# Mixture of experts in a Perceiver kernel: routing of the first layer alone ahead of the tiles, the rest among them

## The reference, cut to what matters

```python
def _route_combine_weights(x_addr, U, k, tau):
    z = x_addr @ U.T
    topv, topi = jax.lax.top_k(z, k)
    w = jax.nn.softmax(topv / (tau + EPS), axis=1)
    ...
    return jnp.zeros((N, L), z.dtype).at[rows, topi].add(w)

def _mixture(inp, C, W):
    for e in range(L):
        y = y + C[:, e:e + 1] * (inp @ W[e].T)
    return y
...
xa = xf @ P_w.T
C1 = _route_combine_weights(xa, U1, K_ROUTE, TAU)
C2 = _route_combine_weights(xa, U2, K_ROUTE, TAU)
C3 = _route_combine_weights(xa, U3, K_ROUTE, TAU)
h = jax.nn.gelu(_mixture(xf, C1, W1), approximate=False)
y = _mixture(h, C2, W2) + C3 @ b2
```

## Time and profile before

| | us |
|---|---|
| three runs, median (lowest to highest) | 1784.96 (1783.38 to 1788.14) |
| the profiled execution, its own time | 1787.54 |
| its span in the profile | 1785.7 |
| busy in the span: PE | 1570.2 (88%) |
| DVE | 1148.1 (64%) |
| ACT | 874.5 (49%) |
| POOL | 683.7 (38%) |
| the stage of the experts, about | 934 to 1039 of the span |

### The profile page before, as it was taken

How to read it: one execution, slowest core, us unless ns; L and a number is a source line. 1 busy time by engine, 2 the same in 40 slices (tenths; PEclk the granted TensorE clock), 3 DMA queues, 4 the chain that set the end, 5 groups by cost and what they waited for, 6 DMA issues and landing times. The chain is left out here.

```text
span 1785.7 us, 42086 instructions
## 1 busy us (share of the span) xinstructions
PE 1570.2 (88%) x15980; PEld 884.5 (50%) x15980; DVE 1148.1 (64%) x1735; ACT 874.5 (49%) x1176; POOL 683.7 (38%) x519
## 2 busy tenths in 40 slices
PE   3999999999499999999765967999999999977772
PEld 1455445545133333334342424777777777763442
DVE  4665665565599999995428647666666666515356
ACT  2555555555077777776240013555555555523430
POOL 2340000000111111111333006999999999943500
PEclk9999999999689999999887988999999999998886
DMA  4787888888432222220300037555555556112000
GB/s 163 198 213 231 210 237 223 223 223 195 139 94 67 64 66 68 64 64 17 153 1 1 1 88 224 140 154 152 153 153 153 153 142 161 28 34 90 1 1 12
DMA packets 178218, 212.19 MB, mean 119 GB/s; under 512 B 57096, under 2 KB 151572, under 8 KB 173486
## 3 DMA queue, kind: packets, MB, share of 16 engines
q1 hardware_dynamic: 177520, 210.45, 42.8%
q10 hardware_dynamic: 576, 0.00, 0.0%
HBM read 122.78 MB, written 87.57 MB: 118 GB/s over the span
## 5 line engine op out<-in xcount | busy, mean ns | idle before, releaser
L1121 POOL TENSOR_TENSOR x_r<-x_p 128x1024 f16<-128x1024 f32 x256 | 479.1, 1894 | 24.1 <-ACT x_p L1097 17.1
L1136 DVE TENSOR_REDUCE x_mx<-a_all 128x2 f32<-128x1024 f32 x249 | 304.9, 1224 | 147.2 <-PE a_all L1020 147.2
L1097 ACT ACTIVATE x_p<-s_all 128x1024 f32<-128x1024 f32 x256 | 248.4, 1022 | 223.2 <-PE s_all L1003 223.2
L702 ACT ACTIVATE x_p<-s_all 128x1024 f32<-128x1024 f32 x256 | 261.3, 1024 | 49.0 <-PE s_all L612 41.8
L757 DVE TENSOR_REDUCE x_mx<-a_all 128x1 f32<-128x512 f32 x352 | 229.4, 681 | 17.2 <-PE o_all L623 8.8
L1003 PE MATMUL s_all<-x_q,x_k 64*128 64x256 f16 x3072 | 210.2, 269 | 0.0
L1038 PEld LDWEIGHTS o_all<-x_v,x_p 128*128 128x128 bf16 x2048 | 178.8, 97 | 40.1 <-issue 40.1
L1038 PE MATMUL o_all<-x_v,x_p 128*128 128x129 f16 x2048 | 197.3, 221 | 0.9 <-POOL x_r L1121 0.9
L1039 PE MATMUL o_all<-x_v,x_r 128*128 128x65 f16 x2048 | 192.5, 193 | 0.0
L1039 PEld LDWEIGHTS o_all<-x_v,x_r 128*128 128x128 f16 x2048 | 180.7, 98 | 0.0
L1003 PEld LDWEIGHTS s_all<-x_q,x_k 64*128 64x128 f16 x3072 | 149.5, 94 | 62.2 <-issue 0.8
(11 more groups left out here) (345 smaller groups left out, 2803.4 us busy)
## 6 DMA issues: line engine op xcount, KB each, us to landing
values<-vst SPq DMA_DIRECT2D x16, 2064.0 KB, 10.4
x_v<-values SPq DMA_DIRECT2D x32, 1032.0 KB, 5.5
keys<-kst SPq DMA_DIRECT2D x32, 1024.0 KB, 6.7
x_k<-keys SPq DMA_DIRECT2D x128, 256.0 KB, 5.2
x_k<-keys SPq DMA_DIRECT2D x192, 64.0 KB, 2.1
values<-vst SPq DMA_DIRECT2D x16, 528.0 KB, 11.5
x_v<-values SPq DMA_DIRECT2D x32, 264.0 KB, 2.6
cf<-in_ctxT SPq DMA_DIRECT2D x16, 512.0 KB, 9.4
```

Source lines behind the costliest of these rows:

```text
L702: act.activation(prob[g % NP][:], chip.s_ps[g % 2][:].rearrange("p (c q) -> p c q", q=SQ), ACT.Exp, scale=hd ** -0.5).then_inc(p_ready, 1)
L1097: act.activation(prob[g % NP][:], chip.s_ps[g % 2][:].rearrange("p (c q) -> p c q", q=SQ), ACT.Exp, scale=hd ** -0.5).then_inc(p_ready, 1)
L1121: pool.tensor_tensor(rest[g % NP][:], prob[g % NP][:], hi, ALU.subtract).then_inc(rest_done, 1)
L1136: dve.tensor_reduce(mx[a[1] % 2][:, n // 4, 2 * (n % 4):2 * (n % 4) + 2], chunk_banks(u, g)[:, :].rearrange("p (h c) -> p h c", h=2), AX.X ...
```

## The change

The weights' split takes pieces: the first layer's in 2 pieces of 3072 numbers, the second's in 8 of 768, each piece a cast and a subtraction. In the experts' block GpSimd first waits until DVE has compared all columns of all routings. ACT rounds `xnT` ahead of copying the address product. The equality and its triangle (a tensor `ew_tri` that was loaded) are gone: an expert is compared with those of lower index by "greater or equal" and with those of higher index by "greater", straight into the rank's tensor, one expert at a time over all its columns. z is laid out by routing, so that the first layer's 4 columns can be taken alone. DVE does these first, and the other 8 columns after the sums of tiles 2 to 7, their rank after tile 8 and their weights after tile 9. PE turns the bias weights after tile 12 and multiplies the biases after tile 14 of the first layer; DVE adds them to x after tile 17. Each token tile of the hidden tensor has a bank of its own: Gelu, transposes, rounding and remainder follow for one token tile as soon as its last sum is there, after tiles 22 and 23 of the first layer and tiles 0 and 1 of the second. The second layer's sums are added into x directly.

Lines that were removed are shown only at the end; the names follow these: `compared`, `weighed` (comparisons; rank and weights), `acc` (sums), `gelu_done`, `h_turned`, `hh_done`, `hl_done` (the hidden tensor's steps), `biased` (x with the biases).

```diff
+    def pieces(self, i):
+        step = 12 * D if i == 0 else 3 * D
+        return [(k, slice(c, c + step)) for k in range(KT) for c in range(0, 12 * D, step)]
+    def parts(self, i):
+        return 2 * len(self.pieces(i))
     def halve(self, pool, i):
-        pool.tensor_copy(self.hi[i][:], self.ws[i][:]).then_inc(self.split, 1)
-        pool.wait_ge(self.split, 2 * i + 1)
-        pool.tensor_tensor(self.lo[i][:], self.ws[i][:], self.hi[i][:], ALU.subtract).then_inc(self.split, 1)
+        done = self.parts(0) if i else 0
+        for k, cs in self.pieces(i):
+            pool.tensor_copy(self.hi[i][:, k, cs], self.ws[i][:, k, cs]).then_inc(self.split, 1)
+            done += 1
+            pool.wait_ge(self.split, done)
+            pool.tensor_tensor(self.lo[i][:, k, cs], self.ws[i][:, k, cs], self.hi[i][:, k, cs], ALU.subtract).then_inc(self.split, 1)
+            done += 1
...
 def experts(chip, tag, weights):
...
             @block.gpsimd
             def _(pool):
+                pool.wait_ge(compared, 2 * L)
                 weights.halve(pool, 1)
...
             @block.tensor
...
+                def tile(i, n):
+                    e, t = tiles[n]
+                    m = i * NTL + n
+                    if m >= 4:
+                        pe.wait_ge(acc, 2 * (m - 3))
+                    if i == 1 and n < NT:
+                        pe.wait_ge(hl_done, n + 1)
+                    for k in range(KT):
+                        ts, es = slice(t * P, (t + 1) * P), slice(e * 2 * D, (e + 1) * 2 * D)
+                        products = ((xh[i], weights.hi[i]), (xh[i], weights.lo[i]), (xl[i], weights.hi[i]))
+                        for q, (a, b) in enumerate(products):
+                            last = pe.matmul(chip.banks[4 + n % 4], a[:, k, ts], b[:, k, es],
+                                             start=(k == 0 and q == 0), stop=(k == KT - 1 and q == 2))
+                    last.then_inc(tile_ready, 1)
+                def turn_bias_weights():
+                    pe.wait_ge(weighed, 10)
                     for t in range(NT):
+                        last = pe.transpose(chip.banks[0][0:L, t * P:(t + 1) * P], cz[:, 2 * NT + t, :], chip.ident[:])
+                    last.then_inc(c3_turned, 1)
+                def biases():
+                    pe.wait_ge(c3_copied, 1)
+                    for t in range(NT):
+                        last = pe.matmul(chip.banks[2 + t // 2][:, (t % 2) * D:(t % 2 + 1) * D], c3T[:, t * P:(t + 1) * P], bb[:],
+                                         start=True, stop=True)
+                    last.then_inc(bias_ready, 1)
+                def turn_hidden(t):
+                    pe.wait_ge(gelu_done, t + 1)
+                    if t >= 2:
+                        pe.wait_ge(biased, 1)
+                    for k in range(KT):
+                        last = pe.transpose(chip.banks[t][:, k * P:(k + 1) * P], hid[:, t, k * P:(k + 1) * P], chip.ident[:])
+                    last.then_inc(h_turned, 1)
+                pe.wait_ge(xl_done, KT)
+                pe.wait_ge(weights.split, weights.parts(0))
+                for n in range(NTL):
+                    tile(0, n)
+                    if n == 12:
+                        turn_bias_weights()
+                    if n == 14:
+                        biases()
+                    if n >= 22:
+                        turn_hidden(n - 22)
+                pe.wait_ge(weights.split, weights.parts(0) + weights.parts(1))
+                for n in range(NTL):
+                    tile(1, n)
+                    if n < 2:
+                        turn_hidden(2 + n)
...
             @block.scalar
                for k in range(KT):
+                    act.activation(xh[0][:, k, :], chip.xnT[:, k, :], ACT.Copy).then_inc(xh_done, 1)
+                act.wait_ge(address_ready, 1)
...
+                def gelu(t):
+                    act.wait_ge(acc, 2 * (NTL - NT + t + 1))
+                    act.activation(hid[:, t, :], y[:, t, :], ACT.Gelu).then_inc(gelu_done, 1)
+                def hidden_high(t):
+                    act.wait_ge(h_turned, t + 1)
+                    act.activation(xh[1][:, :, t * P:(t + 1) * P], chip.banks[t][:, 0:D].rearrange("p (k t) -> p k t", k=KT),
+                                   ACT.Copy).then_inc(hh_done, 1)
+                gelu(0)
+                gelu(1)
+                hidden_high(0)
+                gelu(2)
+                hidden_high(1)
+                gelu(3)
+                hidden_high(2)
+                hidden_high(3)
...
             @block.vector
+                dve.memset(gt[:].rearrange("p c i j -> p c (i j)")[:, :, 0:L * L:L + 1], 0.0)
                 for k in range(KT):
+                    dve.wait_ge(xh_done, k + 1)
+                    dve.tensor_tensor(xl[0][:, k, :], chip.xnT[:, k, :], xh[0][:, k, :], ALU.subtract).then_inc(xl_done, 1)
+                dve.wait_ge(z_ready, 1)
+                dve.tensor_copy(z[:].rearrange("p (r t) l -> p r t l", r=R),
+                                chip.banks[1][:, 0:NC3 * L].rearrange("p (t r l) -> p r t l", r=R, l=L)).then_inc(z_done, 1)
+                dve.wait_ge(z_done, 1)
+                dve.tensor_reduce(mz[:], z[:], AX.X, ALU.max).then_inc(z_done, 1)
+                dve.wait_ge(z_done, 2)
+                dve.tensor_tensor(ez[:], z[:], mz[:].unsqueeze(2).to_broadcast([P, NC3, L]), ALU.subtract).then_inc(z_done, 1)
+                def compare(i, layer):
+                    cs = columns(layer)
+                    n = cs.stop - cs.start
+                    if i > 0:
+                        last = dve.tensor_tensor(gt[:, cs, i, 0:i], z[:, cs, 0:i], z[:, cs, i:i + 1].to_broadcast([P, n, i]), ALU.is_ge)
+                    if i < L - 1:
+                        last = dve.tensor_tensor(gt[:, cs, i, i + 1:L], z[:, cs, i + 1:L],
+                                                 z[:, cs, i:i + 1].to_broadcast([P, n, L - 1 - i]), ALU.is_gt)
+                    last.then_inc(compared, 1)
+                def rank(layer):
+                    cs = columns(layer)
+                    dve.wait_ge(compared, L * (layer + 1))
+                    dve.tensor_reduce(rk[:, cs], gt[:, cs], AX.X, ALU.add).then_inc(weighed, 1)
+                def weigh(layer):
+                    cs, done = columns(layer), 5 * layer
+                    n = cs.stop - cs.start
+                    dve.wait_ge(weighed, done + 1)
+                    dve.wait_ge(exp_done, 1)
+                    dve.scalar_tensor_tensor(out=ez[:, cs], in0=rk[:, cs], scalar=2.5, in1=ez[:, cs], op0=ALU.is_lt,
+                                             op1=ALU.mult).then_inc(weighed, 1)
+                    dve.wait_ge(weighed, done + 2)
+                    dve.tensor_reduce(mz[:, cs], ez[:, cs], AX.X, ALU.add).then_inc(weighed, 1)
+                    dve.wait_ge(weighed, done + 3)
+                    dve.reciprocal(mz[:, cs], mz[:, cs]).then_inc(weighed, 1)
+                    dve.wait_ge(weighed, done + 4)
+                    dve.tensor_tensor(cz[:, cs], ez[:, cs], mz[:, cs].unsqueeze(2).to_broadcast([P, n, L]), ALU.mult).then_inc(weighed, 1)
+                def tile(i, n):
+                    e, t = tiles[n]
+                    m = i * NTL + n
+                    to = (y if i == 0 else chip.x)[:, t, :]
+                    dve.wait_ge(tile_ready, m + 1)
+                    for h in range(2):
+                        src = chip.banks[4 + n % 4][:, h * D:(h + 1) * D]
+                        c = cz[:, i * NT + t, 2 * e + h:2 * e + h + 1]
+                        if i == 0 and e == 0 and h == 0:
+                            dve.tensor_scalar(to, src, c, None, ALU.mult).then_inc(acc, 1)
+                        else:
+                            if i == 1 and e == 0 and h == 0:
+                                dve.wait_ge(biased, 1)
                             else:
                                 dve.wait_ge(acc, 2 * m + h if h else 2 * (m - NT) + 2)
+                            dve.scalar_tensor_tensor(out=to, in0=src, scalar=c, in1=to, op0=ALU.mult, op1=ALU.add).then_inc(acc, 1)
+                def hidden_low(t):
+                    dve.wait_ge(hh_done, t + 1)
+                    ts = slice(t * P, (t + 1) * P)
+                    dve.tensor_tensor(xl[1][:, :, ts], chip.banks[t][:, 0:D].rearrange("p (k t) -> p k t", k=KT),
+                                      xh[1][:, :, ts], ALU.subtract).then_inc(hl_done, 1)
+                for i in range(L):
+                    compare(i, 0)
+                rank(0)
+                weigh(0)
+                dve.wait_ge(weighed, 5)
+                for n in range(NTL):
+                    tile(0, n)
+                    if 2 <= n < 2 + L // 2:
+                        compare(2 * n - 4, 1)
+                        compare(2 * n - 3, 1)
+                    if n == 8:
+                        rank(1)
+                    if n == 9:
+                        weigh(1)
+                    if n == 17:
```

(62 more changed lines are left out.)

87 lines of the change are left out of this document (18 added, 69 removed).

## The result

| | before | changed |
|---|---|---|
| median of 4 runs (lowest to highest), us | 1784.35 (1783.38 to 1788.14) | 1757.9 (1756.57 to 1759.81) |
| ratio, with its 95% interval | | 0.9849 (0.9831 to 0.9867) |
| profiled execution, us (span) | 1787.54 (1785.7) | 1759.81 (1758.0) |
| stage: end of the routing product to the last sum | 939.40 to 1038.55, 99.15 | 938.97 to 1009.12, 70.15 |

The kernel is 26.5 us faster by the medians and 27.7 by the profiled executions; the stage alone is 29.0 shorter. I had forecast 1761, from a stage of 74.9.

A forecast was written before the change was run, and what follows sets the result against it. PE, busy 88% of the span, was taken as the bound. Stage terms 62.2 + 1.0 + 3.5 + 0.6 + 2.7 + 2.0 + 1.7 + 1.2 gave 74.9 against 99.15, so 1761 us, range 1755 to 1771.

The forecast's parts named there:

- Head: Stage start: with GpSimd idle there, PE starts tile 0 at 939.45 without waiting for `moe_xl`, clock taken as high.
- First routing: DVE's path to the first layer's routing weights ends at 944.15, the 22 comparisons taking 2.1 us; before, the path took 14 us.
- Tiles 0 to 12: First-layer tiles with comparisons among DVE's sums: PE may run tile 12 at 957.25, 1.0 us above thirteen tiles' 16.8.
- Bias weights: PE waits 2.0 to 5.0 us, taken 3.5, for DVE's second weighing, two steps of which GpSimd's split can hold.
- Clock again: Behind the bias-weights wait the clock may fall, costing 0 or about 2.7 us; 2.7 taken.
- Biases: The biases' eight passes move from under DVE's last additions onto PE's path: + 2.0 us.
- Between the layers: Hidden tensor's transposes cost 1.7 us, PE does not wait, and GpSimd's split finishes with a cover of 5 us.
- End: Stage end: only one pair of DVE sums remains behind the last tile, 1.2 us.
- The first (sums held by GpSimd): Rival, 6%: 16 GpSimd instructions each hold up one DVE sum, PE stands 13 to 15 us; 1774 to 1776.
- The second (the clock falls while PE meets full banks): Rival, 12%: the clock falls in tiles 4 to 12, costing 10 us at most; 1765 to 1771.
- The third (half clock to the end): Rival, 3%: the clock stays low behind the bias weights from tile 13 on, making the kernel slower; 1803.
- The fourth (short comparisons dear): Rival, 5%: DVE's short-row comparisons cost 0.3 us instead of 0.1, losing the head's gain elsewhere; 1768 to 1772.

The follow-up runs named there:

- the first experiment: The kernel before with one wait added: GpSimd splits the second layer's weights only after DVE has finished all routing; 1770.24 us, ratio 0.9915.
- The experiment with a longer wait: The changed kernel with one or three unused DVE reductions ahead of the second rank, lengthening PE's bias-weights wait; 1758.12 us with one, 1761.53 us with three.
- the last experiment but one: The changed kernel with the biases' product and sum moved back to the stage's end; 1762.97 us, one run, stage 70.34.
- all routings at the head: The changed kernel with all three routings ahead of the first tile's sum, by the new comparisons; 1766.49 us, one run, stage 75.48.

## Why the prediction was right

The time, 1757.9, lies 3 us under the forecast, and each step can be set beside the trace.

- *Head.* Right. Tile 0 began with the routing product's end, and the clock stayed at 1.00. The first experiment shows the cause: with the split out of the way the two remainders take 1.30 us (1.29 in the changed kernel).
- *First routing.* Forecast 4.75 us from the product to the first sum, measured 4.84. The 22 comparisons took 2.1, as worked out from 0.07 us and 1.05 ns a number.
- *Tiles 0 to 12.* I took 1.0 over PE's own time, it was 0.8 from start to start, all of it at the first full bank. I had thought that DVE leads from there on, with 1.46 us a tile and PE meeting a full bank at nearly every one. It did not: from 944.88 to 956.32 PE started 54 matmuls, one every 0.216 us, without a gap. DVE had gained time on tiles 0 and 1, which have no comparisons, and then needed 1.37 a tile. Two sums back to back took 0.92, not the 1.00 read off a stretch in which DVE was waiting for PE; the last end of one pair overlaps the first of the next.
- *Bias weights.* 3.5 taken, 2.38 idle or 2.54 from start to start measured, inside 2.0 to 5.0. The two instructions I named were held, by 0.2 and 0.9.
- *Clock again.* This is the term that was wrong: 2.7 taken, 0 measured. I had called it undecided and taken the dearer end. The experiment with a longer wait gives its price, 2.6, and shows it due at 5.69 us and not at 3.20.
- *Biases.* + 2.0 was right, and the last experiment but one shows that it buys as much at the end.
- *Between the layers.* No wait but the 0.17 at 980.73. Each pair of transposes costs PE 0.22 us (974.28 to 974.72, less the usual 0.216), 0.9 in all; I had taken 1.7, from a row in which eight stand alone. The cover was thinner than said: GpSimd ended at 973.89, PE turned to the second layer at 976.23, 2.3 us later and not 5. A piece took 2.49 us from start to start where I had 2.3: the subtraction 1.64 and not the 1.46 of its like in the earlier trace rows.
- *End.* 1.2, as forecast.

The measured stage is 4.8 below mine, 74.9: 2.7 for the clock, 1.0 for the wait, 0.8 for the hidden tensor's transposes, 0.2 for the tiles, 0.2 for the bias weights' transposes (0.44 where I had 0.6), the rest roundings. I had called all that follows unchanged. Outside the stage 1.3 us by the profiled executions, 2.5 by the medians, went the other way, so that the total came out nearer than its terms; that was luck.

The rivals. The first (sums held by GpSimd) fell: ten of them took 4.64 us beside the pieces. The second (the clock falls while PE meets full banks) did not come true, 1.00 from 944.9 to 957, but it was not tested either: PE met one full bank and none after it. The Trainium skill, TensorE: Matmul & The Clock Gate, section A second HAM failure mode: psum-queue depth-cycling, tells of short idle times between groups of matmuls; this trace has none in that stretch, so it speaks neither for the rule nor against it. The third (half clock to the end) fell too, even behind the wait of 5.69 us, where the clock was back at 1.00 from 965. The fourth (short comparisons dear) fell.

Where the 29.0 came from: four of the kernels form a chain, and the steps between their stages add up.

- 99.15 to 83.40, 15.75: the split's place (the first experiment). 11.9 of it show before tile 4, 0.9 are clock behind the full banks, and 3 are the fall of the clock between the layers, whose cause isn't shown.
- 83.40 to 75.48, 7.9: all else but the place of two routings (from the first experiment to all routings at the head). 3.65 show before tile 4, of which the cheaper comparisons are 3.1. The other 4.3 lie at the change of layers and at the end, where x is added to once instead of twice. Taken out by themselves from the changed kernel, the turning of each token tile at once was worth 2.1 and the biases' place 0.2; the rest I did not separate.
- 75.48 to 70.15, 5.3: two routings among the tiles, with the clock that it saves.

## What to carry to other kernels

- A DVE instruction that reads two SBUF tensors stood here until the end of GpSimd's cast or subtraction: 12 us for a remainder of 512 numbers, 11 for 96 numbers. Look for durations far above the instruction's like and for an end that falls together with GpSimd's. If both must run at once, put GpSimd's work where one of DVE's inputs lies in PSUM, and cut it into pieces (0.8 and 1.6 us here) if DVE has other work among it.
- Work that is needed later goes among the sums as far as DVE has slack: here 0.37 us a tile, and the version that spent it evenly had no stop of PE left but the one at the first full bank. Its stage was 2.3 us shorter, which its total could not show.
- On the bias weights, with PE busy ahead of it, a stop of 2.38 or 3.20 us cost its own length; one of 5.69 cost 2.6 more for the clock. At the change of layers shorter stops were enough, as told below. When two orders differ in one such stop, that term belongs into the range, not into the sum.

## What the runs showed of the hardware that I had not expected

- The same stop, 1.58 us behind eight transposes, was followed by matmuls at half clock in both profiles of the kernel before and at full clock in the first experiment. Another stop of 1.11 us lay ahead of the transposes in all three. So a stretch of partly busy PE may or may not bring the clock down, at 3 us each time.
- GpSimd's subtraction of 768 numbers took 1.64 us with a 16-bit output, 1.46 in the 32-bit one of the earlier trace rows, and the eighth of the large one 1.48 (11.8 / 8): cutting work into eight pieces cost 8 x 2.49 = 19.9 against 17.2 us for the whole.
- A DVE comparison of 4 or 8 numbers is held to the end of GpSimd's instruction like a remainder of 512: it took 1.60 and 0.78 us.
